# Dots a step later, ScalarE's functions a step later, and a third products buffer in a six-phase network kernel

## The chip, the cores and the metric

The kernel runs on 1 core of one Trainium2 chip. The metric is device time in microseconds (us) of one execution. TensorE, VectorE, ScalarE, GpSimd and the queue engine SyncE run their own instruction lists and meet only at semaphores.

## The reference, cut to what matters

The reference applies six blocks to x of shape (32, 16, 16, 192): a state-space layer, a Fourier layer, an attention over chosen keys, a gated mixture of experts, an attention with memory tokens, and a second mixture of experts. The change touches the third alone. There, for each of 32 images of 256 tokens and each of 12 heads of width 16, every token takes the 8 best earlier keys and weighs all sets of one and two of them, together with itself, by the determinant of their Gram matrix:

```python
sim = k @ q_i
sim = jnp.where(jnp.arange(Tn) <= i, sim, -jnp.inf)
_, top_idx = jax.lax.top_k(sim, M)                    # M = 8
...
for comb in COMBS:                                    # 8 singles, 28 pairs
    idx = concatenate([i, top_idx[slots]])
    K, V = k[idx], v[idx]
    gram = jnp.einsum('cnd,cmd->cnm', K, K)
    log_det = jnp.log(jnp.where(valid, det(gram), 1.0) + 1e-06)
    score = log_det / float(s + 1)
    dot = jnp.einsum('cnd,d->cn', K, q_i) / HS ** 0.5
    w = jax.nn.softmax(dot, axis=1)
    out_s = jnp.einsum('cn,cnd->cd', w, V)
...
probs = softmax(scores);  y = probs @ outs            # then y @ W_proj.T + b_proj, added to x
```

## The kernel before, in words

The attention phase is `dpp_attention_phase`. An image is cut into 12 **steps**: steps 0 to 5 serve the first 128 tokens (near, one tile of keys), steps 6 to 11 the second 128 (far, two tiles of keys), each step two heads. All engines run the same list of steps (`steps`), so an engine's order is the order of the statements in its own `body`. The first image is written out, then a hardware loop of 15 passes holds two images each (an odd one, then an even one), and the last image and a tail of 12 steps are written out behind it.

What an index goes through, with q the step's running number:

- Step q: VectorE finds the 8 best scores of two heads (MAX8, FIND_INDEX8, L2529 and L2536). ScalarE casts the indices (`cast_index`, L2205), TensorE turns them (`turn_index`, L2659), ScalarE copies them out of PSUM (`copy_turned`, L2213, the last statement of its step), SyncE writes them to DRAM (L2137) and reads them back broadcast to 128 partitions (`spread`, L2143).
- Step q+2: VectorE compares the spread indices with the key number (L2544, one instruction in near steps, two in far ones) and gets one-hot columns in bf16.
- Step q+3: TensorE gathers keys and values by one-hot matmuls (L2678; 48 in near steps, 96 in far ones), ScalarE copies them from PSUM (`take_gathered`, L2222 to L2224, the first statements of its step), GpSimd makes the products of all pairs of keys (`products`, L2333 to L2339).
- Step q+4: VectorE sums the products to dots (L2553). `prod` has two buffers.

Once per image come the stages of VectorE, each in its own step of the following image: `sim_stage` 0, `denom_stage` 1, `gap_stage` 3, `det_stage` 4, `score_stage` 5, `row_stage` 6, `alpha_stage` 7, the sums of the weighted values in 8 and 9 (`y_stage`, L2512), the residual in 11. Between them stand functions of ScalarE: `differences` (exponential, L2237), `denominators` (logarithm, L2241, with a table load), `gaps` (square, L2245), `logs` (L2249), `weights` (exponential, L2254, with a table load). Each stands in the same step as the VectorE stage that it reads, ahead of `copy_turned`. GpSimd weighs the values in steps 7 and 8 (`weigh`, L2322).

The keys of an image are split in three bf16 parts: high and middle by ScalarE (`split_high`, step 11 of the image before; `split_middle`, step 0), the differences by GpSimd (`split_rest`, 11; `split_low`, 0). `keep_own` (L2232) copies the token's own values in step 1, `normalise` (L112) prepares the next image in step 2, `front` its projections in steps 3 to 10.

## Time and profile before

| | us |
|---|---|
| median of 3 runs | 6864.52 |
| lowest and highest | 6858.64, 6875.67 |
| the profiled execution's own time | 6853.56 |
| its span | 6851.9 |
| VectorE busy | 4293.3 (63%) |
| TensorE matmul busy | 4985.4 (73%) |
| GpSimd busy | 3267.7 (48%) |
| ScalarE busy | 2061.2 (30%) |

The span is the time from the first to the last instruction of the profiled execution; the attention phase lies between about 1590 and 4365 us of it. The engines are called PE (TensorE matmul), PEld (its weight loads), DVE (VectorE), ACT (ScalarE), POOL (GpSimd) and SPq (SyncE's queue) in rows. A name as `l2a_prod<-l2a_keys` is what is written and what is read, `[0.39 <-DMA ...]` behind a row is the idle time of the engine before it and what ended it. "issue" stands for time in which an engine waited for nothing that the profile shows.

### The profile page before, as it was taken

What the parts mean: (1) busy time and instruction counts of PE and PEld (TensorE: products, weight loads), DVE (VectorE), ACT (ScalarE), POOL (GpSimd) and SP (SyncE); (2) the same over time, 40 slices, a digit from 0 to 9 for tenths busy, and PEclk for the clock granted to TensorE, in tenths of its full rate; (3) what the DMA queues carried; (4) which work ended last, traced back from release to release, by engine and by line L of the source; (5) the groups of instructions that cost most, each with busy time, mean ns of one, the idle gap of its engine ahead of it and who ended that gap; (6) DMA issues with size and microseconds to landing.
All of it is one profiled execution on the core that took longest, in us unless ns stands there. A gap on an engine that the chain in (4) does not pass through costs nothing. (4 is left out here: it accounts for less than half of the span.)

```text
span 6851.9 us, 140450 instructions
## 1 busy us (share of the span) xinstructions
PE 4985.4 (73%) x45364; PEld 3654.2 (53%) x45365; DVE 4293.3 (63%) x9002; ACT 2061.2 (30%) x6098; POOL 3267.7 (48%) x4341
## 2 busy tenths in 40 slices
PE   5777776987878888888888888334971997169990
PEld 2333333775555555555555555333850776069990
DVE  5777776227889989999899999723654333212223
ACT  3343333223333333333333333221210332123330
POOL 1222222115667777777777777334235000554447
PEclk8676777997666666666666666557985996589995
DMA  4000000002222222222222222212222002111113
GB/s 140 7 5 5 7 3 6 0 4 73 74 73 75 75 73 76 73 76 75 75 76 73 76 76 74 57 37 72 76 72 60 0 0 61 56 50 45 46 43 110
DMA packets 170739, 369.46 MB, mean 54 GB/s; under 512 B 35650, under 2 KB 100939, under 8 KB 169140
## 3 DMA queue, kind: packets, MB, share of 16 engines
q1 hardware_dynamic: 136404, 283.77, 12.6%
q0 software_dynamic: 33792, 78.69, 3.6%
q8 instruction: 312, 5.11, 0.3%
q14 instruction: 231, 1.89, 0.1%
HBM read 286.86 MB, written 75.50 MB: 53 GB/s over the span
## 5 line engine op out<-in xcount | busy, mean ns | idle before, releaser
L2333 POOL TENSOR_TENSOR l2a_prod<-l2a_keys 128x64 f32<-128x64 f32 (+1 forms) x2304 | 1143.7, 528 | 626.9 <-ACT l2a_norms L2224 619.7
L2678 PE MATMUL l2a_g<-l2a_feat,l2a_onehot 128*128 128x33 bf16 x27648 | 828.3, 187 | 49.4 <-DVE l2a_onehot L2544 24.8
L2678 PEld LDWEIGHTS l2a_g<-l2a_feat,l2a_onehot 128*128 128x128 bf16 x27648 | 807.2, 103 | 57.5 <-DVE l2a_onehot L2544 32.3
L2647 PE MATMUL l2a_s<-l2a_qkT 32*128 32x128 f32 (+1 forms) x1536 | 612.9, 489 | 53.3 <-issue 53.2
L2544 DVE TENSOR_SCALAR l2a_onehot<-l2a_spread,l2a_key_col 128x2048 bf16<-128x2048 bf16 x576 | 545.7, 974 | 141.4 <-DMA l2a_spread<-index_rows 105.1
L1734 POOL TENSOR_TENSOR l_hc<-l_hs,l_bc 128x512 f32<-128x512 f32 x192 | 243.1, 1266 | 794.2 <-DVE l_hs L1808 790.7
L2553 DVE TENSOR_REDUCE l2a_dots<-l2a_prod 128x72 f32<-128x1152 f32 x384 | 515.7, 1343 | 54.2 <-POOL l2a_prod L2339 54.2
L1903 PE MATMUL l_y<-l_hc,l_selT 128*96 128x512 f32 x384 | 308.2, 897 | 294.0 <-POOL l_hc L1734 294.0
L2596 PE MATMUL l2a_a<-l2a_tT,l2a_wqk 96*96 96x256 f32 x1024 | 408.9, 570 | 124.5 <-ACT l2a_tT L2175 124.5
L2222 ACT COPY l2a_keys<-l2a_g 128x128 f32<-128x128 f32 x768 | 199.7, 260 | 816.5 <-PE l2a_g L2678 800.5
L440 POOL DMA_INDIRECT rows_in<-l3f_dispatch_xn,l3f_dispatch_at x128 | 122.9, 960 | 652.5 <-ACT l3f_dispatch_xn L416 613.8
L652 POOL TENSOR_TENSOR l3f_w_own<-l3f_w,l3f_w_own 96x1536 fp32r<-96x1536 f32 x72 | 252.9, 3513 | 326.1 <-DVE l3f_w_own L753 326.1
L2647 PEld LDWEIGHTS l2a_s<-l2a_qkT 32*128 32x128 f32 x1536 | 304.5, 246 | 146.2 <-issue 91.8
L2596 PEld LDWEIGHTS l2a_a<-l2a_tT,l2a_wqk 96*96 96x96 f32 x1024 | 239.9, 248 | 222.0 <-ACT l2a_tT L2175 128.1
L695 PE MATMUL l3f_expert_h<-l3f_tT,l3f_w_own 96*128 96x256 f32 x2592 | 333.9, 288 | 8.9 <-POOL l3f_w_own L652 6.7
L695 PEld LDWEIGHTS l3f_expert_h<-l3f_tT,l3f_w_own 96*128 96x128 f32 x2592 | 320.6, 191 | 9.5 <-issue 7.1
L2339 POOL TENSOR_TENSOR l2a_prod<-l2a_keys,l2a_feat 128x256 f32<-128x256 f32 x384 | 319.9, 833 | 0.0
L759 DVE TENSOR_TENSOR l3f_tT<-l3f_expert_tp,l3f_tT 96x512 fp32r<-96x512 f32 x72 | 49.5, 687 | 421.7 <-ACT l3f_tT L726 421.7
L735 ACT ACTIVATE l3f_hT<-l3f_expert_h,l3f_b 128x256 f32<-128x256 f32 x432 | 181.0, 469 | 380.7 <-PE l3f_expert_h L695 380.7
L710 PE MATMUL l3f_expert_y<-l3f_w,l3f_hT 128*128 x1728 | 292.6, 326 | 0.0
L1808 DVE TENSOR_TENSOR_SCAN l_hs<-l_dA,l_state,l_dBu 128x512 f32<-128x512 f32 x192 | 261.9, 1364 | 39.4 <-ACT l_dA L1684 33.0
L710 PEld LDWEIGHTS l3f_expert_y<-l3f_w,l3f_hT 128*128 128x128 f32 x1728 | 279.1, 190 | 0.0
(403 smaller groups left out, 10979.3 us busy)
## 6 DMA issues: line engine op xcount, KB each, us to landing
l2a_spread<-index_rows SPq DMA_DIRECT2D x384, 512.0 KB, 3.7
rows_in<-main_zeros SPq DMA_DIRECT2D x1, 13824.0 KB, 59.4
l2f_xg<-rows_in SPq DMA_DIRECT2D x72, 192.0 KB, 2.4
rows_out<-l2f_ys POOLq DMA_DIRECT2D x72, 192.0 KB, 2.4
l3f_xg<-rows_in SPq DMA_DIRECT2D x72, 192.0 KB, 2.4
rows_out<-l3f_ys POOLq DMA_DIRECT2D x72, 192.0 KB, 2.4
l3f_w<-in_l3f_w SPq DMA_DIRECT2D x2, 4608.0 KB, 33.9
l_xT<-in_l_xT SPq DMA_DIRECT2D x16, 384.0 KB, 3.8
```

The source lines that it names most:

```text
L652: nc.gpsimd.tensor_tensor(w1_own[:, u, 1, :, :], w1[:, :, bass.ds(e, 1), :].rearrange("p h a f -> p h (a f)"), w1_own[:, u, 0, :, :].bitca ...
L695: ins = nc.tensor.matmul(h_ps[b][:, c % 2, :], w1_own[:, u, wp, h, c * P:(c + 1) * P], tT[:, u, tp_, h, :], start=h == 0 and wp == tp_, st ...
L710: ins = nc.tensor.matmul(y_ps[u][:, t * C:(t + 1) * C], hT[:, u, c, t * P:(t + 1) * P], w2[:, c, bass.ds(e, 1), :].rearrange("p a c -> p ( ...
L1808: nc.vector.tensor_tensor_scan(hs[:, g % 2, :], dA[:, g % 2, :], dBu[:, g % 2, :], state[:, 0, g:g + 1], ALU.mult, ALU.add).then_inc(scan_ ...
L1903: nc.tensor.matmul(y_ps[:, :], selT[:, g, :], hc[:, g % 2, :], start=g == 0, stop=g == G - 1).then_inc(hc_used, 1)
L2333: nc.gpsimd.tensor_tensor(made[:, j, at:at + wide * wide, :].rearrange("p (b a) f -> p b a f", b=wide), key[:, lo:lo + wide, :].unsqueeze( ...
L2339: nc.gpsimd.tensor_tensor(made[:, :, 0:8, :], both, feat[:, u, t, h:h + 4:3, 0:HS].unsqueeze(2).broadcast_to([P, 2, SLOTS, HS]), ALU.mult) ...
L2544: ins = nc.vector.tensor_scalar(onehot[:, s[2] % 2, kt, :, :].rearrange("p k t -> p (k t)"), spread[:, s[2] % 2, :, :].rearrange("p k t -> ...
L2553: nc.vector.tensor_reduce(dots[:, h:h + 4:3, :], prod[:, s[2] % 2, :, :, :], AX.X, ALU.add).then_inc(S["dots_ready"], 1)
L2596: ins = nc.tensor.matmul(o[0:HC, j * T:(j + 1) * T], wqk[:, h, 2 * (k - 1) + j, :], tT[0:HC, h, :], start=h == 0, stop=h == 1)
L2647: nc.tensor.matmul(o, qkT[rows, u, h // 3, t * P:(t + 1) * P], qkT[rows, u, 4 + h // 3, 0:nk], start=True, stop=False, skip_group_check=True)
L2678: ins = nc.tensor.matmul(g_ps[j][:, a * FEAT:(a + 1) * FEAT], onehot[:, s[2] % 2, kt, j * SLOTS + a, :], feat3[:, s[1], kt, piece, h, :], ...
```

## The change

Four things move, and no instruction is added or removed.

1. The five functions of ScalarE stand one step after the VectorE stage that they read. `gap_stage` goes from step 3 to 4, `det_stage` to 5, `score_stage` to 6, `row_stage` to 7; `alpha_stage` stays in 7.
2. Dots are summed in step q+5, ahead of the compares in VectorE's step, and `prod` has three buffers.
3. `split_high` goes from step 11 to step 0, `split_middle` from 0 to 1, `keep_own` from 1 to 2, `split_rest` from 11 to 0, `split_low` from 0 to 1.
4. The waits are changed to match.

```diff
-        prod = m.sb("prod", [P, 2, 2, NCOMB, HS])
+        prod = m.sb("prod", [P, 3, 2, NCOMB, HS])
...
-        SIMS, DENOM, GAP, DET, SCORE, ROWS, ALPHA, VALUE, OUT, PROJECT = 0, 1, 3, 4, 5, 6, 7, 8, 10, 11
-        FRONT, NORMALISE, SQUARE, OWN, SPLIT = 3, 2, 10, 11, 11
+        SIMS, DENOM, GAP, DET, SCORE, ROWS, ALPHA, VALUE, OUT, PROJECT = 0, 1, 4, 5, 6, 7, 7, 8, 10, 11
+        FRONT, NORMALISE, SQUARE, OWN = 3, 2, 10, 11
@@ ScalarE's body
-                    for k, do in ((SIMS, differences), (DENOM, denominators), (GAP, gaps), (DET, logs),
-                                  (SCORE, weights), (OUT, out)):
+                    for k, do in ((SIMS + 1, differences), (DENOM + 1, denominators), (GAP + 1, gaps),
+                                  (DET + 1, logs), (SCORE + 1, weights), (OUT, out)):
                         if previous(n, u, i, k):
                             do(*previous(n, u, i, k))
-                    if i == 1 and not (isinstance(n, int) and n == B):
+                    if i == 0 and real:
+                        split_high(n, u)
+                    if i == 1 and real:
+                        split_middle(n, u)
+                    if i == 2 and real:
                         keep_own(n, u)
...
-                    if nxt and i == SPLIT:
-                        split_high(*nxt)
-                    if i == 0 and real:
-                        split_middle(n, u)
@@ GpSimd's products and body
-                    pool.wait_ge(S["dots_ready"], counted(q - 1) if not (isinstance(q, int) and q < 2) else 1)
-                    made, h = prod[:, s[2] % 2, :, :, :], first_head(s[2])
+                    pool.wait_ge(S["dots_ready"], counted(q - 2) if not (isinstance(q, int) and q < 3) else 1)
+                    made, h = prod[:, s[2] % 3, :, :, :], first_head(s[2])
...
-                    if nxt and i == SPLIT:
-                        split_rest(*nxt)
                     if i == 0 and not (isinstance(n, int) and n == B):
+                        split_rest(n, u)
+                    if i == 1 and not (isinstance(n, int) and n == B):
                         split_low(n, u)
@@ VectorE's body, after MAX8 and FIND_INDEX8
+                    s = back(5)
+                    if s:
+                        q, t = count_of(s), s[2] // PAIRS
+                        dve.wait_ge(S["prod_ready"], counted(q + 1))
+                        h = t * HEADS + first_head(s[2])
+                        nc.vector.tensor_reduce(dots[:, h:h + 4:3, :], prod[:, s[2] % 3, :, :, :], AX.X, ALU.add
+                                                ).then_inc(S["dots_ready"], 1)
                     s = back(2)
...
-                    s = back(4)
-                    if s:
-                        q, t = count_of(s), s[2] // PAIRS
-                        dve.wait_ge(S["prod_ready"], counted(q + 1))
...
```

How the order on the engines changes is shown at three places, all in an odd image in the loop. The first is ScalarE in step 2 before, from the cast of the found indices to the copy of the turned ones:

```order
L2205 CAST l2a_index<-l2a_found 128x16 [waits l2a_turned,l2a_found_ready]
L112 ISA
L112 REGISTER_ALU
L112 ACTIVATE l2a_xn<-main_x_res,l2a_shift,l2a_rstd 128x192
L112 ISA
L112 REGISTER_ALU
L112 ACTIVATE l2a_xn<-main_x_res,l2a_shift,l2a_rstd 128x192
L2210 REGISTER_ALU
L2212 ISA [waits l2a_turned]
L2213 CAST l2a_indexT<-l2a_t 16x128 [waits l2a_rows_out]
```

The same place in the changed kernel, up to the second normalisation, behind which the same three rows follow:

```order
L2205 CAST l2a_index<-l2a_found 128x16 [waits l2a_turned,l2a_found_ready]
L2241 ACT_TABLE_LOAD
L2241 ACTIVATE l2a_denom<-l2a_denom 128x864 [waits l2a_denom_ready]
L2229 REGISTER_ALU
L2232 COPY l2a_values<-l2a_feat 128x12x16 [waits l2a_y_ready]
L2232 COPY l2a_values<-l2a_feat 128x12x16
L112 ISA
L112 REGISTER_ALU
L112 ACTIVATE l2a_xn<-main_x_res,l2a_shift,l2a_rstd 128x192
L112 ISA
L112 REGISTER_ALU
L112 ACTIVATE l2a_xn<-main_x_res,l2a_shift,l2a_rstd 128x192
```

The table load, the logarithm and the two copies of own values have moved in from step 1.

The second is ScalarE in step 1 of the changed kernel, from the second pair of gathered keys on:

```order
L2222 COPY l2a_keys<-l2a_g 128x128 [waits l2a_gathered]
L2223 COPY l2a_values<-l2a_g 128x128
L2224 COPY l2a_norms<-l2a_g 128x8
L2203 ISA
L2205 CAST l2a_index<-l2a_found 128x16 [waits l2a_turned,l2a_found_ready]
L2237 ACTIVATE l2a_ex<-l2a_ex 128x1056 [waits l2a_diff_ready]
L2198 CAST l2a_feat<-l2a_rest_f 128x2x396 [waits l2a_rest_ready]
L2210 REGISTER_ALU
L2212 ISA [waits l2a_turned]
L2213 CAST l2a_indexT<-l2a_t 16x128 [waits l2a_rows_out]
```

The exponential (L2237) and the middle split (L2198) stood in these places of step 0 before; the exponential is now behind the gathered keys of step 1.

The third is VectorE in step 1, before:

```order
L2536 MAX_INDEX l2a_found<-l2a_sims,l2a_s 128x8 [waits l2a_max_chain]
L2541 ISA
L2542 ISA [waits l2a_spread_in]
L2544 TENSOR_SCALAR l2a_onehot<-l2a_spread,l2a_key_col 128x2048 [waits l2a_gathered]
L2544 TENSOR_SCALAR l2a_onehot<-l2a_spread,l2a_key_col 128x2048
L2553 TENSOR_REDUCE l2a_dots<-l2a_prod 128x2x36 [waits l2a_prod_ready]
L2408 TENSOR_TENSOR l2a_denom<-l2a_ex 128x24x8 [waits l2a_exp_ready]
```

And the same place in the changed kernel, whose line numbers are two lower or a few higher:

```order
L2534 MAX_INDEX l2a_found<-l2a_sims,l2a_s 128x8 [waits l2a_max_chain]
L2541 TENSOR_REDUCE l2a_dots<-l2a_prod 128x2x36 [waits l2a_prod_ready]
L2546 ISA
L2547 ISA [waits l2a_spread_in]
L2549 TENSOR_SCALAR l2a_onehot<-l2a_spread,l2a_key_col 128x2048 [waits l2a_gathered]
L2549 TENSOR_SCALAR l2a_onehot<-l2a_spread,l2a_key_col 128x2048
L2406 TENSOR_TENSOR l2a_denom<-l2a_ex 128x24x8 [waits l2a_exp_ready]
```

The dots have gone ahead of the wait for the spread indices, and the denominators, which need the exponential, follow the compares directly.

## Rows read from the trace of the kernel before

**Rows 1.** stretch of the attention phase: length, busy us (PE, PEld, DVE, ACT, POOL)

```profile
1590.00:4365.00 2775.00, 2258.03 (x32492) 1620.88 (x32490) 2510.65 (x5135) 953.54 (x3972) 1983.94 (x3259) 0.66 0.22 75
```

**Rows 2.** VectorE's compares and dots (page's part 5), then min/median/max ns

```profile
L2544 DVE TENSOR_SCALAR l2a_onehot<-l2a_spread,l2a_key_col 128x2048 bf16<-128x2048 bf16 x576 | 545.7, 974 | 141.4 <-DMA l2a_spread<-index_rows 105.1 <-PE l2a_g L2678 35.8
L2553 DVE TENSOR_REDUCE l2a_dots<-l2a_prod 128x72 f32<-128x1152 f32 x384 | 515.7, 1343 | 54.2 <-POOL l2a_prod L2339 54.2
...
L2544 DVE TENSOR_SCALAR l2a_onehot<-l2a_spread,l2a_key_col x576: 723/804/2374, 1595.3 to 4350.4; 128x2048 bf16<-128x2048 bf16 x192
```

**Rows 3.** waits in the phase (who, for whom: us in total, times, longest)

```profile
ACT l2a_keys L2222 <- PE l2a_g L2678: 800.5, 393, 8.4
...
DVE l2a_onehot L2544 <- DMA l2a_spread<-index_rows: 105.1, 58, 4.5
...
DVE l2a_dots L2553 <- POOL l2a_prod L2339: 54.2, 40, 3.2
PE l2a_s L2647 <- issue: 53.2, 14, 4.0
...
DVE l2a_onehot L2544 <- PE l2a_g L2678: 35.8, 22, 2.9
...
POOL l2a_prod L2333 <- DVE l2a_dots L2553: 2.3, 1, 2.3
```

**Rows 4.** timeline, head of a loop pass (start us, duration us, engine, what)

```profile
2862.60 1.99 DVE L2544 TENSOR_SCALAR l2a_onehot<-l2a_spread,l2a_key_col 128x2048 bf16<-128x2048 bf16 x2
...
2865.22 0.79 PE L2647 MATMUL l2a_s<-l2a_qkT 32*128 32x128 f32 x2 [3.63 <-issue]
...
2868.68 2.90 PE L2678 MATMUL l2a_g<-l2a_feat,l2a_onehot 128*128 128x33 bf16 x96 [1.52 <-issue]
...
2868.81 0.29 DVE L2536 FIND_INDEX8 l2a_found<-l2a_sims,l2a_s 128x8 uint32<-128x128 f32 x1
...
2871.62 1.77 DVE L2544 TENSOR_SCALAR l2a_onehot<-l2a_spread,l2a_key_col 128x2048 bf16<-128x2048 bf16 x2 [2.52 <-PE l2a_g L2678]
...
2872.10 1.11 ACT L2237 ACTIVATE l2a_ex<-l2a_ex 128x1056 f32<-128x1056 f32 x1
...
2876.69 0.23 ACT L2205 CAST l2a_index<-l2a_found 128x16 bf16<-128x16 uint32 x1
```

**Rows 5.** timeline, ScalarE's table load and logarithm

```profile
2530.61 1.28 ACT L2241 ACT_TABLE_LOAD   x1
...
2531.90 0.92 ACT L2241 ACTIVATE l2a_denom<-l2a_denom 128x864 f32<-128x864 f32 x1
```

**Rows 6.** timeline, steps 2 and 3 of an even image

```profile
2617.92 0.48 DVE L2529 MAX8 l2a_sims<-l2a_s 128x8 f32<-128x128 f32 x2
...
2618.72 0.29 DVE L2536 FIND_INDEX8 l2a_found<-l2a_sims,l2a_s 128x8 uint32<-128x128 f32 x1
...
2618.86 0.61 ACT L2232 COPY l2a_values<-l2a_feat 128x192 f32<-128x192 f32 x2
...
2619.37 0.25 ACT L2213 CAST l2a_indexT<-l2a_t 16x128 bf16<-16x128 f32 x1
...
2619.72 0.32 SPq L2137 DMA_DIRECT2D index_rows<-l2a_indexT  x1
...
2620.46 1.00 ACT L112 ACTIVATE l2a_xn<-main_x_res,l2a_shift,l2a_rstd 128x192 f32 x2
...
2621.05 0.33 SPq L2143 DMA_DIRECT2D l2a_spread<-index_rows  x1
...
2624.58 0.82 DVE L2544 TENSOR_SCALAR l2a_onehot<-l2a_spread,l2a_key_col 128x2048 bf16<-128x2048 bf16 x1 [1.81 <-DMA l2a_spread<-index_rows]
```

**Rows 7.** timeline, compares beside GpSimd's weighting, steps 8 and 9

```profile
2661.70 3.13 POOL L2322 TENSOR_TENSOR l2a_values<-l2a_values,l2a_alpha 128x1728 f32<-128x1728 f32 x1 [3.98 <-DVE l2a_alpha L2503]
...
2663.01 3.10 DVE L2544 TENSOR_SCALAR l2a_onehot<-l2a_spread,l2a_key_col 128x2048 bf16<-128x2048 bf16 x2
...
2671.81 1.89 DVE L2544 TENSOR_SCALAR l2a_onehot<-l2a_spread,l2a_key_col 128x2048 bf16<-128x2048 bf16 x2
```

5 lines of the change are left out of this document (removed).

## The prediction

> **What bounds the kernel now.** I read the stretches first, then the groups of VectorE by cost, the table of waits, and the timeline of two images. The attention phase takes 2775 of the 6852 us, and in it VectorE is busy for 2511, TensorE for 2258, GpSimd for 1984, ScalarE for 954 [rows 1]. Nothing outside this phase is touched. VectorE is thus the engine nearest to full, and what shortens the phase is what shortens VectorE's own sequence: its work and its waits. Among its groups stand 576 compares (onehot) of 974 ns mean, 723 at best, and 384 sums of products (dots) of 1343 ns [rows 2]. The waits that the change is about: before the compares 105.1 us for the broadcast of the indices and 35.8 for TensorE's gathers, before the dots 54.2 for GpSimd's products [rows 3]. Together 195.1 us in 31 or so images, 6.3 per image of about 87.
>
> Where do they come from? In step 0 and step 1 ScalarE waited for the stage that VectorE computes at the end of the same step, and only then copied the turned indices that the DMAs need. The second source is the loop. Every second image starts a pass of it, and there TensorE stands still: 3.63 us before the scores and 1.52 before the gather, without a releaser [rows 4]; the table has 14 of the first kind, 53.2 us [rows 3]. By the loop there are 15 passes and one exit, so I count 16 such images (odd ones) and 15 to 16 even ones. In the odd image shown, VectorE's compare waited 2.52 us for the gather [rows 4].
>
> **The change part by part.** It adds no work: the same instructions on each engine, so only waits and collisions count.
>
> *What goes.* With each ScalarE function a step later than the stage it reads, it no longer waits for VectorE, and the index copy follows its cast directly in most steps. The dots, a step later, read products finished about 7 us earlier, and standing before the compare they fill 1.27 us (1.34 with its overlap) of a compare's wait. I let all three waits go: -195.1 us. Bounds: all, or, if the slow chain only moves, none.
>
> *What is late next, at the head of the loop.* The exponential of the differences now stands in step 1, behind the copies of the gathered keys and the cast of step 1, and VectorE's denominators in the same step need it. Before, it ran at 2872.10, well ahead. In the odd image the cast of step 1 starts at 2876.69 [rows 4]; it hangs on the gather, thus on TensorE's standstill, which the change leaves as it is. Exponential: cast 0.2 and 1.1, ready at 2878.0. VectorE: the last index of step 1 is found at 2868.81 + 0.29 = 2869.1, dots to 2870.4, a wait of 1.2 for the gather until 2871.6, compares to 2873.4 [rows 4], then a wait of 4.6 until 2878.0. Behind this wait stand the denominators and the whole of step 2. Sum 5.8 us in 16 images: +93. In even images there is no standstill of 3.63 + 1.52 = 5.2 us, which is more than 4.6, so I let the dots and the two compares cover the exponential there. Bounds: 0, if TensorE gets ahead; 16 x (8.4 + 1.2) = 154, by ScalarE's longest wait for a gather, 8.4 [rows 3].
>
> *What is late next, in step 2.* Between the cast and the copy of the turned indices ScalarE had only the normalisation. Now the table load and logarithm (1.28 + 0.92 [rows 5]), the kept values (0.61) and the normalisation (1.00 [rows 6]) stand there. The chain for the index of step 2: 0.2 cast, 3.8 for those, then from copy to compare 5.2 (copy at 2619.37, DMA out at 2619.72, broadcast at 2621.05, the waiting compare at 2624.58 [rows 6]); in all 9.2 us after the index is found. VectorE needs it in step 4. Till there it has dots 1.27, compare 0.65, then finding 1.09 (2617.92 to 2619.01 [rows 6]), dots, compare, finding, dots: 2 x (1.27 + 0.65 + 1.09) + 1.27 = 7.3. Wait: 1.9 us in 31 images, +59. Behind it stand the gap stage and all later steps. Bounds: 0, and 124 (4.0 each, if nothing of the added 2.8 and of a late cast is covered). The chains of steps 0, 1 and 3 are as long or shorter, but steps with a stage of 2 to 5 us lie in between, so they are covered.
>
> *The second exponential.* It was computed at the end of step 5 and read in step 6; now it is computed and read in step 7. After the found index ScalarE needs 0.2 + 1.28 + 0.92 = 2.4 [rows 5], VectorE's dots and compare 1.27 + 0.65 = 1.9: wait 0.5 x 31 = +16 (bounds 0 and 62, were it 2 us). The rows and alpha stages now fall into one step, which is no work more. GpSimd's weighting starts after alpha as before, and its 3.13 us are covered by finding, dots and compares of step 8 (over 4 us) before VectorE sums the values.
>
> *Third buffer and moved splits.* Products waited 2.3 us in all for a free buffer [rows 3], and with three buffers and dots one step later they may run exactly as far ahead as before; 0. The high part of the split goes from step 11 to 0, its rest on GpSimd likewise, the middle and low parts to step 1; TensorE reads them from step 3 on, some 8 us after. 0, covered by steps 1 and 2 of VectorE (bounds 0 and 31, one us per image).
>
> *Compares against GpSimd.* 576 x (974 - 723 ns) = 145 us of the compares is more than their least time [rows 2]. In step 8 two compares issued at 2663.01 took 3.10 us, while GpSimd's weighting ran from 2661.70 to 2664.83 [rows 7]: the first ended 0.55 us after it, 1.64 above two undisturbed ones (1.46). With the dots ahead the compare is issued at 2664.3, with only 0.5 left to wait out: the first takes 1.05, 1.3 us less. In step 9 the same, smaller (two took 1.89, so 0.43 to gain at most [rows 7]). Elsewhere it moves into the middle of the products, whose instructions are short: nothing either way. I take -1.5 per image, -46. Bounds: -145, all collisions gone, and +78. The latter is from two compares that met products in step 0 and took 1.99 us, 0.995 each [rows 4]: were all so, and 0.11 on top for the weightings' collisions as now (31 x 2.1 us over 576), the mean would be 1.11 us, 576 x (1.11 - 0.974) = 78.
>
> The trace so agrees with what the Trainium skill says in "SBUF — State Buffer", section Who interferes with whom: a tensor_scalar in its fast mode and a GpSimd instruction exclude each other on the shared ports, the later one blocking entirely, while a tensor_reduce never takes them. By that rule the dots, a reduce, are what should overlap the weighting, as above.
>
> Sum: -195.1 + 93 + 59 + 16 - 46 = **-73 us**. The profiled execution took 6853.6 us (span 6851.9), 11 below the median of the runs, 6864.5. 6853.6 - 73 = 6780.6; I go a third of the way to the median's scale, as one profile is one run, and forecast **6784 us**. Its own range, without the other cases, is 6720 to 6845.
>
> **A rule that speaks against it.** On ScalarE a table load and its function stand back to back: load at 2530.61 for 1.28, logarithm at 2531.90, 0.01 between [rows 5]. The Trainium skill ("ScalarE: Activation LUTs", section What ACT_TABLE_LOAD costs) adds to each load a drain of about 1.38 us. By the page's figure, an estimate, the waits of step 4 and step 7 would each grow by 1.4 us in 31 images, +86, and the change would bring nothing. The row shows no such drain, so I hold to the row.
>
> **The rivals.**
> (A) *The waits go and none comes.* TensorE, no longer held by late casts, enters the loop's head earlier, and the broadcast is quicker than in my chain. For it: the gathers themselves are only 2.9 us long, TensorE is idle for 517 of 2775 us. Against: the order of turning output, front, projection and gathers from step 10 on hangs on VectorE's value sums, which do not move. Time: 6853.6 - 195 - 46 + 16 = 6628; with the median's offset about 6635.
> (B) *The waits only change place.* Step 4 waits 3 us, because the cast of step 2 is itself late behind the gathers (93 instead of 59), and the compares keep their collisions (0 instead of -46): -73 + 34 + 46 = +7, 6861, about 6866 on the median's scale. For it: ScalarE waited 800.5 us for gathers, in 393 places [rows 3], and every cast is behind such copies. Against: in step 2 the gather has 6 us since the one before.
> (C) *Slower: the compares run into the products.* Issued 1.3 us later in each step, each compare meets GpSimd inside its products rather than in the gap ahead of them. The new waits leave only -195.1 + 168 = -27, so slower by over 21 us begins where the mean compare exceeds 974 + (27 + 21) / 576 x 1000 = 1057 ns. At the 1.11 us of the bound it is -27 + 78 = +51: 6905, or 6915 on the median's scale. For it: GpSimd is busy 1984 of 2775 us. Against: the largest collisions, those with the weighting, shrink.
>
> **How the numbers follow.** Chances: forecast 0.55, A 0.12, B 0.20, C 0.13. What a measurement of this kernel can tell from no change is 0.3%, 21 us, so the lines are at 6844 and 6885. Faster: 0.52 of the forecast, A's 0.12, 0.03 of B, together 0.67. Same: 0.03 of the forecast, 0.15 of B, 0.03 of C, 0.21. Slower: 0.02 of B and 0.10 of C, 0.12. The range that should hold it 8 times in 10 leaves out A and most of C: 6680 to 6875.
>
> **What would show it.** In the changed profile: the dots' wait for products near 0; the compares' wait for the broadcast near 60 us, nearly all in step 4, and for gathers near 20; a new wait of the denominators (or of VectorE before them) for ScalarE's exponential of about 75 us in 16 places of 4 to 5 us, none in even images; about 15 us before the row sums; a mean compare near 890 ns. ScalarE's waits for VectorE's stages (gap, det, score) should be gone. I am wrong if denominators wait in every image, if step 4 does not wait, or if the mean compare rises.

## The result, and the profile after

| | before | after |
|---|---|---|
| median of 10 runs each, us | 6861.47 | 6881.32 |
| lowest and highest | 6846.64 to 6876.1 | 6863.23 to 6896.15 |
| the profiled execution's own time | 6853.56 | 6863.23 |
| its span | 6851.9 | 6861.6 |

The ratio is 1.0026, with a 95% interval of 1.0015 to 1.0036: the change costs 10 to 25 us, where a gain of 77 was forecast. Between the two profiled executions the difference is 9.7 us. The one of before stands 8 us below the median of its kernel, the one of after 18 us.

The attention phase starts 9.5 us later in the second trace, though the code ahead of it is the same: the first score search is at 1585.85 us before and at 1595.31 after. So the stretch of the phase is read here from this instruction to VectorE's last one of the phase, first before, then after (columns as in rows 1).

```profile
1585.85:4396.17 2810.32, 2264.49 (x32512) 1625.35 (x32512) 2532.90 (x5183) 960.55 (x3983) 1992.31 (x3262) 0.66 0.22 74
```

```profile
1595.31:4413.89 2818.58, 2271.45 (x32512) 1628.79 (x32512) 2526.72 (x5183) 988.98 (x3983) 1998.89 (x3262) 0.66 0.22 74
```

The phase is 8.3 us longer; what lies ahead of it is 9.5 longer and what lies behind it 8.0 shorter, so only 8 of the medians' 20 us are seen at the change. In the fourteen profiled executions of this document the first score search lies anywhere from 1586 to 1609 us, with the same code ahead of it, and where the rest of the 20 us comes from stays open. Inside the phase VectorE is busy 6.2 us less (2532.90 to 2526.72) and not busy 14.4 us more (277.4 to 291.9). The granted clock of TensorE is 0.66 in both. Of the forecast's two halves, then, the work did get shorter, but by 6 us and not by 46, and the waits did not shrink by 27 but grew by 14.

The waits in the phase (who, for whom: us in total, times, longest).

```profile
DVE l2a_onehot L2549 <- DMA l2a_spread<-index_rows: 87.1, 39, 3.9
DVE l2a_denom L2406 <- ACT l2a_ex L2237: 85.8, 20, 5.6
...
DVE l2a_sums L2471 <- ACT l2a_det L2254: 14.8, 31, 0.6
DVE l2a_sims L2527 <- PE l2a_s L2647: 12.8, 8, 3.6
DVE l2a_onehot L2549 <- PE l2a_g L2676: 12.7, 10, 1.9
```

These answer to [rows 3]. The 54.2 us before the dots are gone. Two waits that were not there have come: the denominators for ScalarE's exponential, 85.8, and the row sums, 14.8. The broadcast's 87.1 looks like the old 105.1, but it stands elsewhere: 80 us of it lie in step 4, 2.5 in each of the 32 images, where the compare of step 2's indices stands; before, 97 of the 105 lay in steps 2 and 3. Together 201.4 (with 1.0 left before the dots), against 195.1. The rest of the added idle time is mostly before the score searches: their waits, of which the `l2a_sims` row shows one, come to 42.2 us before and 49.3 after.

The compares and the dots in the page's list of groups, and the compare's least, median and longest time in ns.

```profile
L2549 DVE TENSOR_SCALAR l2a_onehot<-l2a_spread,l2a_key_col 128x2048 bf16<-128x2048 bf16 x576 | 527.0, 941 | 99.8 <-DMA l2a_spread<-index_rows 87.1
...
L2541 DVE TENSOR_REDUCE l2a_dots<-l2a_prod 128x72 f32<-128x1152 f32 x384 | 511.5, 1332 | 1.0 <-POOL l2a_prod L2338 1.0
```

```profile
L2549 DVE TENSOR_SCALAR l2a_onehot<-l2a_spread,l2a_key_col x576: 732/806/3318, 1602.9 to 4371.0; 128x2048 bf16<-128x2048 bf16 x192
```

The compares cost 18.7 us less than in [rows 2], the dots 4.2. Since VectorE as a whole is busy only 6.2 less, its other instructions take about 17 more; of images 1 to 30 alone, its TENSOR_TENSOR instructions take 16.4 us more. The groups that carry this, first of before, then of after (same columns; each is a stage's instruction with two inputs in VectorE's memory):

```profile
L2438 DVE TENSOR_TENSOR l2a_det<-l2a_det,l2a_minor 128x96 f32<-128x96 f32 x93 | 41.8, 500 | 0.0
L2410 DVE TENSOR_TENSOR l2a_denom<-l2a_denom,l2a_ex 128x96 f32<-128x96 f32 x96 | 40.0, 468 | 1.1
...
L2441 DVE TENSOR_TENSOR l2a_denom<-l2a_denom,l2a_veto 128x432 f32<-128x432 f32 x31 | 33.2, 1072 | 0.0
...
L2425 DVE TENSOR_TENSOR l2a_gap<-l2a_ratio,l2a_dots 128x96 f32<-128x96 f32 x96 | 19.9, 261 | 0.0
```

```profile
L2408 DVE TENSOR_TENSOR l2a_denom<-l2a_denom,l2a_ex 128x96 f32<-128x96 f32 x96 | 61.3, 690 | 1.1
...
L2423 DVE TENSOR_TENSOR l2a_gap<-l2a_ratio,l2a_dots 128x96 f32<-128x96 f32 x93 | 34.9, 427 | 0.0
L2436 DVE TENSOR_TENSOR l2a_det<-l2a_det,l2a_minor 128x96 f32<-128x96 f32 x93 | 28.6, 360 | 0.0
...
L2439 DVE TENSOR_TENSOR l2a_denom<-l2a_denom,l2a_veto 128x432 f32<-128x432 f32 x31 | 18.5, 596 | 0.0
```

The same instruction takes 468 ns in one kernel and 690 in the other. What it stands beside has changed, as the timeline of an odd image shows: it is the head of a loop pass, as [rows 4] of before, some 15 us later in the span, 9.5 of them from the later start (start us, duration us, engine, what; in brackets the idle time before it and what ended it).

```profile
2891.87 0.23 ACT L2205 CAST l2a_index<-l2a_found 128x16 bf16<-128x16 uint32 x1
2891.98 1.11 ACT L2237 ACTIVATE l2a_ex<-l2a_ex 128x1056 f32<-128x1056 f32 x1
```

```profile
2886.27 1.47 DVE L2549 TENSOR_SCALAR l2a_onehot<-l2a_spread,l2a_key_col 128x2048 bf16<-128x2048 bf16 x2
2893.11 0.85 DVE L2406 TENSOR_TENSOR l2a_denom<-l2a_ex 128x192 f32<-128x192 f32 x1 [5.38 <-ACT l2a_ex L2237]
2894.00 3.33 DVE L2408 TENSOR_TENSOR l2a_denom<-l2a_denom,l2a_ex 128x96 f32<-128x96 f32 x4
```

```profile
2894.25 0.71 POOL L2338 TENSOR_TENSOR l2a_prod<-l2a_keys,l2a_feat 128x256 f32<-128x256 f32 x1
2894.92 1.71 POOL L2313 TENSOR_TENSOR l2a_feat<-l2a_rest_f,l2a_feat 128x792 bf16<-128x792 f32 x1
2896.59 2.84 POOL L2332 TENSOR_TENSOR l2a_prod<-l2a_keys 128x64 f32<-128x64 f32 x6
```

The exponential is late behind the cast, as forecast, and VectorE waits 5.38 us. Then its four denominators take 3.33 us, beside a long instruction of GpSimd (the low split, 1.71). The same holds over images 1 to 31: in the 19 where the low split runs beside them they take 3.32 us on average, in the other 12 they take 1.85. In the same image of before, as in all of before, they took 1.84, beside GpSimd's short products:

```profile
2877.18 1.84 DVE L2410 TENSOR_TENSOR l2a_denom<-l2a_denom,l2a_ex 128x96 f32<-128x96 f32 x4
```

```profile
2876.90 3.00 POOL L2333 TENSOR_TENSOR l2a_prod<-l2a_keys 128x64 f32<-128x64 f32 x6
```

Steps 2 to 4 of that image, the chain of the index of step 2 (it answers [rows 6]):

```profile
2898.39 0.20 ACT L2205 CAST l2a_index<-l2a_found 128x16 bf16<-128x16 uint32 x1 [1.66 <-DVE l2a_found L2534]
2898.61 1.28 ACT L2241 ACT_TABLE_LOAD   x1
2899.90 0.92 ACT L2241 ACTIVATE l2a_denom<-l2a_denom 128x864 f32<-128x864 f32 x1
...
2902.13 0.24 ACT L2213 CAST l2a_indexT<-l2a_t 16x128 bf16<-16x128 f32 x1
...
2903.82 0.33 SPq L2143 DMA_DIRECT2D l2a_spread<-index_rows  x1
```

```profile
2907.76 1.07 DVE L2549 TENSOR_SCALAR l2a_onehot<-l2a_spread,l2a_key_col 128x2048 bf16<-128x2048 bf16 x1 [2.17 <-DMA l2a_spread<-index_rows]
```

From the cast to the copy 3.7 us, from the copy to the compare 5.6, and the compare waits 2.17. Over images 1 to 30 the means are 3.75 and 5.9 us (5.4 to 7.3), and the cast starts 0.13 us after the index is found: it is not late.

**A balance per image.** For the experiments I split VectorE's time in images 1 to 30, from the records of every one of its instructions: its idle time, and the excess of each instruction over the least time of its form (the first percentile over all kernels here). The least times add up to 81.3 us an image, of which 13 are the overlap of neighbours, so time = 68.3 + idle + excess, within 0.3. Each row comes from one execution. That of after is 18 us under the median of its kernel, that of loop_of_four 14 us over it; 15 us are 0.5 us an image, and differences of that size between rows say little. Means over the 30 images, us:

```
                 image   idle   excess: compares   others
before           87.16   7.58           4.48        6.70
after            87.48   8.29           3.76        7.25
turn_first       86.77   6.08           3.96        8.50
exp_first        87.79   7.77           4.30        7.33
both_first       85.63   4.51           4.11        8.75
dots_behind      89.09   9.65           5.11        5.94
dots_alone       88.46   5.87           5.83        8.56
scalar_alone     88.04   6.78           5.14        7.79
loop_of_four     86.99   6.93           4.21        7.71
best_guess       86.57   3.11           4.85       10.54
both_loop4       85.87   3.46           4.55        9.70
narrow_before    82.02   8.13           3.24        2.48
narrow_after     81.85   9.03           1.05        3.82
narrow_both      79.12   5.85           1.68        3.44
```

### The profile page after: what moved, and what is told of

It reads as the page before. It is cut to its first block and busy times, and to the rows that moved or that the text cites. A ratio compares the mean times of both kernels' runs of the same rounds, so it can differ in the third digit from the quotient of the medians.

```text
span 6861.6 us, 140135 instructions
## 1 busy us (share of the span) xinstructions
PE 5001.4 (73%) x45364; PEld 3659.8 (53%) x45365; DVE 4288.2 (62%) x9002; ACT 2090.7 (30%) x6098; POOL 3274.0 (48%) x4341
## 3 DMA queue, kind: packets, MB, share of 16 engines
q1 hardware_dynamic: 136404, 283.77, 12.7%
## 5 line engine op out<-in xcount | busy, mean ns | idle before, releaser
L2332 POOL TENSOR_TENSOR l2a_prod<-l2a_keys 128x64 f32<-128x64 f32 (+1 forms) x2304 | 1170.9, 539 | 534.6 <-ACT l2a_norms L2224 532.8
L2645 PE MATMUL l2a_s<-l2a_qkT 32*128 32x128 f32 (+1 forms) x1536 | 622.8, 497 | 53.5 <-issue 34.2
L2549 DVE TENSOR_SCALAR l2a_onehot<-l2a_spread,l2a_key_col 128x2048 bf16<-128x2048 bf16 x576 | 527.0, 941 | 99.8 <-DMA l2a_spread<-index_rows 87.1
L2541 DVE TENSOR_REDUCE l2a_dots<-l2a_prod 128x72 f32<-128x1152 f32 x384 | 511.5, 1332 | 1.0 <-POOL l2a_prod L2338 1.0
L2594 PE MATMUL l2a_a<-l2a_tT,l2a_wqk 96*96 96x256 f32 x1024 | 373.8, 530 | 0.7 <-ACT l2a_tT L2175 0.7
L2657 PE MATMUL l2a_t<-l2a_ident_bf,l2a_index 128*16 128x128 bf16 x384 | 96.0, 250 | 367.2 <-ACT l2a_index L2205 366.6
L2321 POOL TENSOR_TENSOR l2a_values<-l2a_values,l2a_alpha 128x1728 f32<-128x1728 f32 x64 | 200.4, 3131 | 265.0 <-DVE l2a_alpha L2501 265.0
L2657 PEld LDWEIGHTS l2a_t<-l2a_ident_bf,l2a_index 128*16 128x16 bf16 x384 | 33.1, 86 | 522.7 <-ACT l2a_index L2205 457.3
L2338 POOL TENSOR_TENSOR l2a_prod<-l2a_keys,l2a_feat 128x256 f32<-128x256 f32 x384 | 301.0, 784 | 0.0
```

Of the source, the lines that this page charges most:

```text
L2332: nc.gpsimd.tensor_tensor(made[:, j, at:at + wide * wide, :].rearrange("p (b a) f -> p b a f", b=wide), key[:, lo:lo + wide, :].unsqueeze( ...
L2338: nc.gpsimd.tensor_tensor(made[:, :, 0:8, :], both, feat[:, u, t, h:h + 4:3, 0:HS].unsqueeze(2).broadcast_to([P, 2, SLOTS, HS]), ALU.mult) ...
L2541: nc.vector.tensor_reduce(dots[:, h:h + 4:3, :], prod[:, s[2] % 3, :, :, :], AX.X, ALU.add).then_inc(S["dots_ready"], 1)
L2549: ins = nc.vector.tensor_scalar(onehot[:, s[2] % 2, kt, :, :].rearrange("p k t -> p (k t)"), spread[:, s[2] % 2, :, :].rearrange("p k t -> ...
L2594: ins = nc.tensor.matmul(o[0:HC, j * T:(j + 1) * T], wqk[:, h, 2 * (k - 1) + j, :], tT[0:HC, h, :], start=h == 0, stop=h == 1)
L2645: nc.tensor.matmul(o, qkT[rows, u, h // 3, t * P:(t + 1) * P], qkT[rows, u, 4 + h // 3, 0:nk], start=True, stop=False, skip_group_check=True)
```

## The experiments

Ratios are to the kernel before, run beside each on the same chip, with 95% intervals. The median of before was 6857 to 6873 us in these groups of runs, so a difference to after is given by the ratios (that to 1.0026, of 6861 us) and not by the medians. All edits are on the kernel after unless said otherwise; the cuts of code are shortened, and a function that is moved is shown where it comes to stand.

**turn_first: the copy of the turned index first in step 2.** ScalarE's order in `body`:

```diff
-                    for k, do in ((SIMS + 1, differences), (DENOM + 1, denominators), (GAP + 1, gaps),
+                    for k, do in ((SIMS + 1, differences), (GAP + 1, gaps),
...
-                    if i == 2 and real:
-                        keep_own(n, u)
...
                     if real:
                         copy_turned(n, u, i)
+                    if nxt and i == NORMALISE:
+                        normalise(...)
+                    if previous(n, u, i, DENOM + 1):
+                        denominators(*previous(n, u, i, DENOM + 1))
+                    if i == 2 and real:
+                        keep_own(n, u)
```

> The changed kernel, with ScalarE's copy of the turned indices of step 2 ahead of the table load, logarithm, kept values and normalisation. Theory V (VectorE's own waits set the phase): the compares' wait of step 4 for the broadcast (about 73 of 87 us in 30 images) goes to under 10 us, and the time falls by 55 to 75 us against the changed kernel, to 6806 to 6826. Rival T (TensorE's sequence sets the phase, VectorE's waits only mirror it): the wait reappears as a wait for gathers or scores and the time stays within 15 us of 6881. Rival G (collisions of compares with GpSimd take the place of the wait): the wait goes, but the mean compare rises from 941 to over 1000 ns, and less than half is gained.

Measured: 6850.73, ratio 0.9987 [0.9973, 1.0001]. In its trace:

```profile
DVE l2a_denom L2408 <- ACT l2a_ex L2237: 73.6, 18, 5.5
...
DVE l2a_onehot L2551 <- DMA l2a_spread<-index_rows: 13.1, 15, 2.5
```

The broadcast's wait falls from 87.1 to 13.1, so without the logarithm, the kept values and the normalisation ahead of the copy it does not come (scalar_alone below shows what else it needs). The time falls by 27 us, not by the 55 to 75 expected: the balance shows idle -2.2 us an image and other instructions +1.25. The mean compare is 951 ns, so rival G's sign of it does not come, though less than half is gained.

**exp_first: the exponential first in step 1.**

```diff
                     real, s3 = not (isinstance(n, int) and n == B), back(3)
+                    if previous(n, u, i, SIMS + 1):
+                        differences(*previous(n, u, i, SIMS + 1))
                     if s3:
                         take_gathered(s3, 0)
...
-                    for k, do in ((SIMS + 1, differences), (DENOM + 1, denominators), (GAP + 1, gaps),
+                    for k, do in ((DENOM + 1, denominators), (GAP + 1, gaps),
```

> The changed kernel, with the exponential of the differences as the first work of ScalarE in step 1, ahead of the copies of gathered keys. Theory V: the 85.8 us that VectorE's denominators waited for it go; since they then meet TensorE sooner, some of it comes back at the head of the loop, so the time falls by 50 to 86 us, to 6795 to 6831. Rival T: the wait is merely moved to the compares and score searches of steps 1 and 2, gain under 20 us. Rival G: gain under 40 us with a mean compare over 1000 ns.

Measured: 6873.28, ratio 1.0025 [1.0013, 1.0036].

```profile
DVE l2a_onehot L2551 <- DMA l2a_spread<-index_rows: 118.0, 55, 4.9
...
DVE l2a_dots L2543 <- POOL l2a_prod L2340: 12.4, 11, 1.3
```

The denominators' wait falls from 85.8 to 10.1 us, so the gather's copies ahead of the exponential were its cause. Nothing clear of noise is gained, where 50 to 86 us were expected: what VectorE no longer loses at the head of the image it loses in steps 3 and 4, before the broadcast (87.1 to 118.0) and before the dots (12.4, new). It comes there earlier, and the index of step 2 does not: its cast starts 2.1 us after the index is found, against 0.13 in after, as ScalarE is still behind the gathers. The two waits are in a row on one chain.

**both_first: both moves.** The two edits above together.

> Both edits, exponential first in step 1 and copy of turned indices first in step 2. Theory V: the gains add, 105 to 160 us below the changed kernel, 6721 to 6776, faster than the kernel before by 1.2 to 2%. Rival T: one bound replaces the other, at most 40 us. Rival G: 40 to 90 us, mean compare over 1000 ns.

Measured: 6815.08, ratio 0.9946 [0.9926, 0.9966]. It is faster than either kernel, and the two moves together give 55 us where one gives 27 and the other 1. The 105 to 160 expected are missed; the time is that of rival G, but the mean compare is 954 ns and not over 1000. What is left of the waits:

```profile
DVE l2a_onehot L2553 <- DMA l2a_spread<-index_rows: 38.5, 39, 2.7
...
DVE l2a_dots L2545 <- POOL l2a_prod L2342: 16.9, 14, 2.1
DVE l2a_sums L2475 <- ACT l2a_det L2254: 15.5, 32, 1.0
...
DVE l2a_denom L2410 <- ACT l2a_ex L2237: 10.1, 14, 0.7
```

Against after, idle falls by 3.78 us an image and the excess grows by 1.85: half of what the waits give is given back as longer instructions. One rival stays open: the granted clock of TensorE over 1590 to 4375 us is 0.66 in after, 0.68 in turn_first and 0.69 in both_first, where TensorE is busy 82 us less (2271.72 to 2189.49). VectorE's wait for gathers differs by 2 us only (12.7 and 10.4), but how much the clock adds along the index's way, and whether it is a cause or comes of the other order, was not separated.

**dots_behind: the dots behind the compares again**, a step later as in the kernel after; only the block's place in VectorE's step differs.

```diff
-                    s = back(5)
-                    if s:
...
                     s = back(2)
...
+                    s = back(5)
+                    if s:
...
```

> The changed kernel with one thing undone: the dots stand behind the compares again (still a step later, three buffers). Theory V: the compares' waits for broadcast and gathers grow by up to 1.27 us in each of the 31 images in step 4 (+39 us) and in 16 odd ones in step 1 (+20, partly inside the wait for the exponential, so +0 to +20); the compares beside the weighting in step 8 cost 1.2 us more (+38): 40 to 90 us slower than the changed kernel, 6920 to 6970. Rival T and rival G: within 15 us of it, or faster because the compares meet idle GpSimd time again (mean compare 970, dots and compares otherwise free to swap).

Measured: 6910.68, ratio 1.0082 [1.0066, 1.0099]: 38 us slower than after, at the edge of the 40 to 90 expected, and not within the 15 of the rivals. The mean compare is 1009 ns instead of 941. The compares' excess is 1.35 us an image higher, close to the 1.5 that the forecast gave the dots' place; the other instructions' excess is 1.31 lower, and that takes it back. What is lost is idle time, 1.36 us an image.

**dots_alone: the dots' part without ScalarE's.** On the kernel before: three buffers, `back(5)` ahead of the compares, and the stages that read dots a step later; ScalarE and the splits as they were.

```diff
-        prod = m.sb("prod", [P, 2, 2, NCOMB, HS])
+        prod = m.sb("prod", [P, 3, 2, NCOMB, HS])
...
-        SIMS, DENOM, GAP, DET, SCORE, ROWS, ALPHA, VALUE, OUT, PROJECT = 0, 1, 3, 4, 5, 6, 7, 8, 10, 11
+        SIMS, DENOM, GAP, DET, SCORE, ROWS, ALPHA, VALUE, OUT, PROJECT = 0, 1, 4, 5, 6, 7, 7, 8, 10, 11
```

> One part of the change alone on the kernel before: dots one step later, three buffers, dots ahead of the compares, VectorE's stages in steps 4, 5, 6, 7, 7; ScalarE's functions stay in the step of the stage that they read, the splits stay. Account theory (VectorE's time = its least work + its waits + its collisions with GpSimd, and about half of a removed wait comes back as collisions): the 54 us for products go, of the 105 for the broadcast about 50 are filled by the dots, the weighting's collision loses 1.25 us per image (38): 140 us off, 50 to 70 back: 6775 to 6815. Rival (each part costs by itself, the two gaps of the change are in this part): 6860 to 6890.

Measured: 6895.16, ratio 1.0054 [1.0040, 1.0067], a miss by 80 us or more. The waits did what was expected of them: none for products, 10.3 for gathers. But

```profile
DVE l2a_onehot L2551 <- DMA l2a_spread<-index_rows: 124.2, 82, 4.3
```

```profile
L2551 DVE TENSOR_SCALAR l2a_onehot<-l2a_spread,l2a_key_col 128x2048 bf16<-128x2048 bf16 x576 | 588.2, 1047 | 134.6 <-DMA l2a_spread<-index_rows 124.2
```

Idle is 1.7 us an image lower than before, and the excess 3.2 higher, 1.35 of it in the compares, whose mean rises from 974 to 1047 ns. That is what rival C forecast, and a kernel with the dots ahead of the compares: in step 8, beside the weighting, they take 39 us less than in before, in the other steps together 81 more.

**scalar_alone: ScalarE's part without the dots'.** After, with two buffers, `back(4)` behind the compares and the stages at 3, 4, 5, 6, 7.

```diff
-        prod = m.sb("prod", [P, 3, 2, NCOMB, HS])
+        prod = m.sb("prod", [P, 2, 2, NCOMB, HS])
...
-                    s = back(5)
-                    if s:
...
                     s = back(2)
...
+                    s = back(4)
+                    if s:
...
```

> The other part alone on the kernel before: ScalarE's five functions, the splits and the kept values a step later; two buffers, dots in step q+4 behind the compares, stages in steps 3 to 7 as before. Account theory: the wait for the exponential (70 to 90 us) and the one for the broadcast, now in step 4 (100 to 130, without the dots in front), replace the old ones for the broadcast (105), and the wait for products (54) stays: 6890 to 6930, so this part is the one that costs. Rival: it gives what the other part loses, under 6860.

Measured: 6886.18, ratio 1.0039 [1.0023, 1.0054], just under the 6890 to 6930 expected.

```profile
DVE l2a_dots L2551 <- POOL l2a_prod L2338: 65.3, 38, 1.9
DVE l2a_onehot L2542 <- PE l2a_g L2676: 39.2, 25, 2.9
DVE l2a_denom L2406 <- ACT l2a_ex L2237: 29.6, 14, 2.3
...
DVE l2a_onehot L2542 <- DMA l2a_spread<-index_rows: 10.1, 8, 2.2
```

ScalarE's part takes the broadcast's wait away almost whole (105.1 to 10.1), where 100 to 130 us in step 4 were expected, and leaves those for gathers and products, which the dots' part takes. Only 1.9 us of it stand in step 4, although ScalarE's load is that of after: from the cast to the copy of step 2's index it is 3.75 us on average here too. What differs is VectorE: here the gap stage is in step 3, ahead of the compare that needs the index, and it takes 4.9 us (2626.70 to 2631.58 in before). From copy to compare 8.5 us pass without a wait. In after the gap stage stands in step 4 behind that compare, because the dots come a step later. So the wait of step 4 has two causes that only meet in the whole change, ScalarE's load ahead of the copy and the gap stage's move out of step 3. Idle is 0.8 us an image below before's, the excess 1.75 above. Each part alone makes the kernel slower by more than both together (0.54%, 0.39% and 0.26%): their effects do not add (the last two intervals overlap), and in both the loss lies in the excess, not in the waits.

**loop_of_four: four images in a pass.**

```diff
-            with eng.Fori(0, B // 2 - 1) as it:
-                image(it * 2 + 1, 1)
-                image(it * 2 + 2, 0)
+            with eng.Fori(0, 7) as it:
+                image(it * 4 + 1, 1)
+                image(it * 4 + 2, 0)
+                image(it * 4 + 3, 1)
+                image(it * 4 + 4, 0)
+            image(29, 1)
+            image(30, 0)
```

> The changed kernel with four images in a pass of the loop (7 passes, then 29, 30 and 31 written out), so TensorE's standstill comes 8 times and not 16. Account theory: the odd images' idle of 10.7 us falls to the even ones' 5.9 in 8 of them, 39 us, half of it given back: 15 to 39 us off, 6842 to 6866, and the wait for the exponential falls from 86 to about 50. Rival (the standstill comes from the code's place in memory or length, not from the pass): as many standstills as before, 6881 unchanged.

Measured: 6843.63, ratio 0.9967 [0.9954, 0.9979].

```profile
PE l2a_s L2649 <- issue: 20.1, 5, 4.3
PE l2a_s L2649 <- DVE l2a_found L2538: 3.7, 1, 3.7
```

```profile
DVE l2a_denom L2410 <- ACT l2a_ex L2241: 45.9, 13, 5.5
```

TensorE's standstill comes with the pass of the loop: with 7 passes it is 23.8 us in 6 places, where [rows 3] has 53.2 in 14 and after 53.5 in 15 (34.2 for nothing that the trace shows, 19.3 put down to the found index; 14 of them of 3.5 us or more). The places are images 5, 9, ... 25 here and 3, 5, ... 29 in before and after. So it comes at each jump back to the head of the loop, one time fewer than there are passes; the first pass and the code behind the loop have none. The wait for the exponential falls to about half (85.8 to 45.9). The broadcast's wait stays (89.2 against 87.1), as it should, since neither of its causes is touched. The time falls by 40 us and is inside the expected band; the balance shows less, its execution being 14 us over the median.

**best_guess: both moves, the loop of four, and the row sums' functions (`weights`) first in step 7.**

```diff
+                    if previous(n, u, i, SCORE + 1):
+                        weights(*previous(n, u, i, SCORE + 1))
                     if s3:
                         take_gathered(s3, 0)
```

> Everything that points forward: the changed kernel with both exponentials first in ScalarE's step, the copy of turned indices first in step 2, and four images in a pass. On top of both_first (6815): the 15 us before the row sums go, and odd images' idle of 6.2 us falls to 2.8 in 8 of them (27), half given back in collisions: 6785 to 6805. Rival (what is left is set by TensorE and GpSimd, and a further wait removed brings nothing): 6808 to 6822.

Measured: 6821.25, ratio 0.9930 [0.9910, 0.9949]. Its idle time is the lowest of all, 3.11 us an image, and its excess the highest, 15.4; its time is in the rival's band, no better than both_first.

**both_loop4: the same without the move in step 7.**

> Both moves of ScalarE's work (both_first) and the loop of four images a pass, without the third move of best_guess (row sums first in step 7). By the theory that a removed wait is paid in full: both_first lost 66 us against after's 6881, the loop of four 38; together some 104, so 6777 us, ratio 0.989. By the theory that VectorE's time is least work + waits + collisions with GpSimd, and that each wait removed comes back by about half as collisions once VectorE runs denser: the waits left in both_first are 6.2 us in an odd image and 2.8 in an even one, the longer loop takes at most 3.4 off eight of the images, 27 us, and half of it returns: 6800, between 6785 and 6815. If best_guess's move of the row sums did not matter, the time is its 6821 again. I hold to 6800.

Measured: 6810.44, ratio 0.9912 [0.9893, 0.9931]: inside the band of the second theory, and the fastest of all kernels in full, 78 us under after and 62 under before. By the balance it gives nothing over both_first: idle -1.05 us an image, excess +1.4. The intervals of the two overlap, so whether the longer loop is worth anything here stays open.

**narrow_before and narrow_after: GpSimd's products over 2 of 16 features.** The other 14 are left out and stay 0, so the dots are not the reference's; the number of instructions is the same, but for one that sets the buffer to 0 at the start of the phase. One kernel is before, the other after.

```diff
-                                made[:, j, at:at + wide * wide, :].rearrange("p (b a) f -> p b a f", b=wide),
+                                made[:, j, at:at + wide * wide, 0:2].rearrange("p (b a) f -> p b a f", b=wide),
```

> The kernel before, with GpSimd's products over 2 of the 16 features (the other 14 are zero in the buffer, so the dots are wrong; VectorE's work is the same). It takes GpSimd's busy time down to a third and with it the collisions, in which VectorE spends about 11.1 us per image above its least times (compares 4.5, its other instructions 6.6). Account theory: 5 to 8 us per image of the collisions go and the 54 us of waits for products, waits for the broadcast remain: 200 to 300 us less than before, 6560 to 6660. Rival (collisions are hidden, TensorE bounds): under 80 us less.

> The same on the changed kernel: GpSimd's products over 2 of 16 features, dots wrong, VectorE's work the same. Account theory: collisions fall by 5 to 8 us per image here too (of 10.9), but no wait for products is there to go: 150 to 250 us less than 6881, 6630 to 6730, with the waits for the exponential and for the broadcast of step 4 in place or longer. So it stays slower than the narrowed kernel before. My first reckoning (the change lowers collisions by itself): then it would be the faster one of the two with GpSimd at full work, and level here.

Measured: 6689.25, ratio 0.9744 [0.9722, 0.9767], and 6676.36, ratio 0.9724 [0.9701, 0.9748]. Stretches and compares of both, before first (the phase is shorter here, hence its end at 4185):

```profile
1590.00:4185.00 2595.00, 2206.71 (x32334) 1588.47 (x32335) 2317.11 (x5108) 955.07 (x3961) 1058.91 (x3239) 0.68 0.25 80
```

```profile
1590.00:4185.00 2595.00, 2161.22 (x32480) 1569.47 (x32480) 2296.91 (x5137) 981.15 (x3974) 1122.87 (x3254) 0.71 0.25 81
```

```profile
L2550 DVE TENSOR_SCALAR l2a_onehot<-l2a_spread,l2a_key_col 128x2048 bf16<-128x2048 bf16 x576 | 437.9, 788 | 119.2 <-DMA l2a_spread<-index_rows 98.6 <-PE l2a_g L2677 20.5
```

GpSimd's busy time is about halved, and VectorE, whose instructions are the same, is busy some 200 us less: the excess falls from 11.2 to 5.7 us an image in before and from 11.0 to 4.9 in after. So the excess is for its greater part the price of GpSimd beside it. The waits do not shrink (idle +0.55 and +0.74). The kernel before loses 176 us, less than the 200 to 300 expected; the narrowed after is inside its 6630 to 6730. I had expected after to stay the slower of the two; it is not, the intervals overlap.

**narrow_both: both_first with the narrow products.**

> both_first with GpSimd's products over 2 of 16 features (14 of 16 left out, set to 0, so that the sums of products are not the reference's); to be read beside narrow_after (6676 us), which is the changed kernel with the same products. In full width the two moves took 66 us off and the idle time of VectorE fell by 3.8 us per image (some 118 us), so about 50 came back as longer instructions. If what comes back is collisions with GpSimd, then with GpSimd light the idle time removed is paid in full or nearly: idle of narrow_after is 12.3 in odd and 5.7 in even images, its two new waits (exponential, index of step 2) hold about the same 5 to 7 us of an odd and 2 of an even image, so 80 to 120 us less than narrow_after: 6560 to 6600. If instead VectorE's instructions lengthen for a reason of their own (denser issue), half is given back here too: 6615 to 6640. The first is my theory.

Measured: 6620.51, ratio 0.9624 [0.9605, 0.9644]. The time is outside my band and in the rival's, 56 us under narrow_after, or 69 by the ratios (0.9724 - 0.9624 of 6865). The balance says why, and bears out the first theory's mechanism: idle falls by 3.18 us an image, 95 in 30 images, where I had reckoned with 80 to 120, and the excess grows by 0.25 where it grew by 1.85 in full width. The phase is 82 us shorter in 30 images, 86% of the idle time removed, against 55 of 113 us (49%) in full width. The rest of the difference to the medians lies outside the phase or between runs, and was not settled.

## Why the prediction was wrong

It forecast -73 us on the trace's own scale; the phase grew by 8, and the two executions differ by 10. Point by point:

- **What bounds the phase**: borne out. With GpSimd's products narrowed, VectorE's busy time in the phase fell by 194 us (before) and 204 (after), and the kernels' time, by the ratios, by 176 and 207. TensorE's own busy time fell by less, 51 and 111 (2258.03 to 2206.71, 2271.72 to 2161.22).
- **What goes, -195.1**: the dots' wait went (54.2 to 1.0), ScalarE's own waits for the stages gap, det and score too, and of the broadcast's old waits 7 us are left. Right.
- **The loop's head, +93**: right in mechanism and place. The denominators waited 5.0 us in 14 odd images (4.6 in 16 forecast: the standstill comes with the 14 jumps back) and also 2.8 in five even ones (none forecast); 85.8, with 12.7 before gathers 98.5. exp_first and loop_of_four show both causes, the gather's copies ahead of the exponential and the standstill at the pass.
- **Step 2, +59**: right in mechanism, shown by turn_first, and mis-sized: 80 us were measured, 2.5 in each of 32 images. Cast to copy is 3.75 us, as reckoned, but copy to compare took 5.9 on average where I took 5.2 from one place. The sum's 7.3 us of VectorE's way to the compare have no stage in them, which is the other half of the cause, as scalar_alone shows; the prediction named ScalarE's load alone.
- **The second exponential, +16**: 14.8. **Third buffer and splits, 0**: the buffer costs no wait. The low split, however, now stands beside the denominators of step 1 (below).
- **Compares against GpSimd, -46**: this is the step that failed. Its local part came true: in step 8 of the image shown below the compares take 1.84 us behind the weighting instead of 3.10 [rows 7]. Over all images the compares of step 8 are 39 us shorter, where 1.3 us an image, 40, were reckoned. The sum did not come. In the other steps, where I wrote "nothing either way", the compares take 20 us more, so that they are 18.7 us shorter in all and not 46. And VectorE's other instructions, above all those with two inputs, are 17 us longer: the denominators (+21.3 for one form, 468 to 690 ns) and the gap's (+15.0, 261 to 427) more than det's and the veto's (-13.2 and -14.7) give back. For these the prediction had no term at all. With the dots' 4.2 less the net is -6.

The compares by step, us over all images:

```
step            0     1     2     3     4     5     6     7      8     9    10    11
before       71.2  51.1  28.6  29.5  23.8  23.5  23.6  26.8  100.4  62.2  69.2  51.0
after        51.3  62.4  27.4  25.6  28.3  28.9  25.4  27.5   61.6  62.7  85.0  56.2
dots_alone   66.4  74.1  26.7  30.9  32.1  29.3  36.8  33.9   61.3  62.6  91.1  57.9
```

After the change, in the timeline of step 8 of one image:

```profile
2941.20 3.13 POOL L2321 TENSOR_TENSOR l2a_values<-l2a_values,l2a_alpha 128x1728 f32<-128x1728 f32 x1 [7.88 <-DVE l2a_alpha L2501]
...
2943.76 1.84 DVE L2549 TENSOR_SCALAR l2a_onehot<-l2a_spread,l2a_key_col 128x2048 bf16<-128x2048 bf16 x2
```

The sum as measured: waits -195.1 + 201.4 = +6, other idle time +8 (14.4 less 6.3), 7 of it before the score searches, work -6: +8. The forecast had -27 and -46, so 41 us of the error are idle time and 40 are work. None of the large waits is of a kind that I had not named; together they came a fifth larger than reckoned (201 for 168), and each of my sizes was read at a single image.

Rival B, whose waits of 3 us in step 4 and unchanged collisions gave +7 and 6866, came nearest: the waits did only change place. That its +7 stands beside the phase's +8 is in part luck. Step 4 waited 2.5 us and not 3; the compares did not keep their time but lost 18.7 us, and instructions that B does not name took 17 back. B's own reason, a cast of step 2 late behind the gathers, is not what happened: that cast starts 0.13 us after the index is found. ScalarE's waits for gathers did grow from 800.5 us to the row below, but it no longer waits for VectorE's stages, and that time went to its waits for gathers and for found indices.

```profile
ACT l2a_keys L2222 <- PE l2a_g L2676: 1097.8, 532, 9.0
```

The two parts of TensorE's standstill in the table of waits of after:

```profile
PE l2a_s L2645 <- issue: 34.2, 10, 4.3
PE l2a_s L2645 <- DVE l2a_found L2534: 19.3, 5, 4.1
```

Rival C's mean compare over 1057 ns did not come (941), but its mechanism is seen in dots_alone (1047). Rival A, in which no wait comes, fails: 201 us of them came, and TensorE stood still at the loop's head as before (53.5 us against 53.2).

What the forecast lacked is an account that the balance shows: where VectorE waits less beside a GpSimd at work 72% of the phase, its instructions grow. From after to turn_first the excess takes back 66% of the idle time removed, to both_first 49%, from before to dots_alone and to scalar_alone more than all, so the share is no constant. With GpSimd light, in the one pair of kernels that was run (narrow_after and narrow_both), it is 8%. This is shown for the sum; which pairs of instructions meet was followed only at the places above.

The rule of the Trainium skill that I leaned on ("SBUF — State Buffer", section Who interferes with whom) says more than I took from it: apart from a tensor_scalar in its fast mode, a VectorE instruction with two inputs in SBUF contends with a GpSimd instruction that reads SBUF, while a tensor_reduce never contends. The runs agree on the reduce: the dots take 1332 to 1345 ns on average in all kernels, narrow ones too. They agree on the instructions with two inputs as well, and that was in the trace of before (468 ns on average for a form that takes 272 in narrow_before; the column of other instructions is 6.70 us an image, that of compares 4.48), and I did not read it. As to the rule that spoke against the change ("ScalarE: Activation LUTs", What ACT_TABLE_LOAD costs), the trace of after differs from it as that of before did: load at 2898.61 for 1.28, logarithm at 2899.90, no drain of 1.38 us between them. The wait of step 4 is explained without it.

## What to carry to other kernels

Where two engines collide, do not count a removed wait at its full length (both_first kept half of it, the other pairs with GpSimd at full work less), and price a moved stage by what the other engine executes beside it, for every instruction with two inputs and not only for the group that is largest. When an engine's order is shifted, look for the producer that now stands between an index and its DMA, or between a gather's copies and a function that something waits for: here two such places made 166 us of waits, and moving them ahead turned a loss of 0.26% into a gain of 0.54%. Look too at what the waiting engine no longer has to do on its way there: a stage that is moved behind the reader takes away the cover (scalar_alone). Waits that hang on one late engine are in series: removing the first alone (exp_first) moves it to the next place. And before two traces are compared over a fixed window, see whether the phase starts at the same time in both.
